# Second attention: rows of queries, keys, sums and low output halves moved by DMA in place of products; out projection in two passes

## Chip, core and metric

The kernel runs on one core of one Trainium2 chip. The metric is the device time of one execution in microseconds; the median of the runs shown counts.

## The reference

The model is a stack of four residual blocks on x of 2 x 1024 tokens x 256 features. The change concerns the third, a causal attention of 16 heads of 16 features:

```python
def _L1_attn_ref(x, w_attn, b_attn, w_proj, b_proj):
    ...
    qkv = x @ w_attn + b_attn
    q, k, v = jnp.split(qkv, 3, axis=-1)
    ...
    q, k, v = (heads(q), heads(k), heads(v))
    scale = 1.0 / np.sqrt(HEAD_DIM).astype(np.float32)
    att = jnp.einsum('bhqd,bhkd->bhqk', q, k) * scale
    causal = jnp.tril(jnp.ones((Tlen, Tlen), dtype=bool))
    att = jnp.where(causal, att, -jnp.inf)
    att = jax.nn.softmax(att, axis=-1)
    y = jnp.einsum('bhqk,bhkd->bhqd', att, v)
    y = y.transpose(0, 2, 1, 3).reshape(Bsz, Tlen, Cdim)
    return y @ w_proj + b_proj
...
x = x + _layernorm(_L1_attn_ref(_layernorm(x, axis=-1), L1_attn_w_attn, L1_attn_b_attn, L1_attn_w_proj, L1_attn_b_proj), axis=-1)
```

The other blocks are an attention of 16 heads of 128 features, a gated feed-forward layer and a mixture of 16 experts. All is in fp32.

## The kernel before

A product with fp32 precision is made of reduced operands: each number is split into a high part (type float32r) and a low part, the rest, and `three_passes` (L78) adds high x high, low x high and high x low. The stages follow each other in blocks, one instruction list per engine, with semaphores between them written by hand. Each engine runs its list in order, so a wait holds all that stands behind it.

The second attention is `attention1_stage` (L1425). Work is cut into 8 **halves**: four heads (`HG`) of one batch. A half has two **chunks** c of 512 queries, and 12 **quads** (c, kt), each the four heads' scores of one chunk against 128 keys. Every engine has a function `step(g)` for the quad g; r = g mod 12 is the step in the half, and `small_work` (L1456) says which small jobs stand at the end of which step, as (kind, half relative to the present one, chunk, part). The steps go from -4 to TOTAL + 10.

What a step does on TensorE (L2002): scores of quad g + 1 for one pair of heads (L1936), the maxima products of unit g + 10 (`maxima`, L1615), weighing v with the exponentials of quad g (`weigh_v`, L1940), then the same for the other pair of heads, then the small jobs (`small`, L1965). Scores and small jobs share a ring of four PSUM banks, maxima use three, o has one. ScalarE takes the exponentials (L2023) and copies o (L2030); GpSimd masks the diagonal quads (`hide_later`, L1870) one step ahead of their weighing; VectorE takes maxima out of PSUM (`take_max`, L1651).

The maxima pass runs one half ahead: unit 0 of the next half stands at r = 2, unit 4 (the first of chunk 1) at r = 6. The small jobs of one half and chunk, in order:

- `project` (L1596): queries and keys of four heads, 128 rows x 512 tokens, six products. ScalarE copies the high part (L1636), VectorE makes the low part (L1648). It stands at r = 11 for chunk 0, two halves ahead, and at r = 3 for chunk 1.
- `stack` (L1602), four per chunk: the scores' operands hold, per head of a pair, high, low and again high (or high, high, low) rows of 16 features above each other, so that one product does all three passes. Two products with a 0/1 matrix `to_stack` place the rows; ScalarE copies them (L1641, L1644). At r = 0, 1 and r = 4, 5.
- `shift` (L1609): the negated maxima are placed in further rows of q and added by VectorE (L1686), at r = 8 and r = 2.
- `sums` (L1985): the sum of exponentials is in o below each head's 16 rows; products with a selector bring it to 128x16, VectorE inverts it (L2094), GpSimd widens it (L1897), `spread` (L1991) transposes it back and ScalarE copies the factor (L2056).
- `make_y` (L1841), GpSimd: multiply o by the factor, high part, low part. Its three instructions stand in three steps (`Y_AFTER`, L1469), with maskings between them.
- `out` (L1994), two per chunk: three passes against the output weights; VectorE adds to the accumulator (L2100).

The first half's projections, stacks and first maxima are made in the block of the first feed-forward layer, at the steps of `early_jobs` (L1476). SP's queue carries only loads here: weights and biases of a half (L1577), constants (L1693).

## Time and profile before

| what | value |
|---|---|
| median of 3 runs | 2309.24 us (2307.34 to 2699.71) |
| profiled execution | 2301.61 us |
| its span | 2299.9 us |
| second attention in the span | 1526 to 1926 us, preparation from 1507 |
| mean granted TensorE clock | 0.962 |
| TensorE, VectorE, ScalarE, GpSimd busy | 2141.7, 1507.0, 1176.5, 541.1 us |

How to read the rows below. A row of a table of stretches has the stretch in us from the span's start, its length, then the busy time (and number of instructions) of TensorE's products, TensorE's weight loads, VectorE, ScalarE and GpSimd, then the granted clock as a share of full speed, the DMA share and GB/s. A timeline row has start, duration, engine (PE TensorE, PEld its weight loads, DVE VectorE, ACT ScalarE, POOL GpSimd, SPq the queue of SP), the line, the operation, what it writes and reads, the shapes, how many are merged in the row, and in brackets the idle time before it and what ended it. Products are pipelined: durations overlap, so what a group costs is read from its start to the start of the next. A row of a group has the count, busy us and mean ns, and the idle time before. In the timeline of TensorE below, steps begin with their first scores (L1936): r = 7 at 1718.49, r = 0 at 1737.42, r = 2 at 1745.54, r = 3 at 1749.20, r = 5 at 1760.12, r = 7 at 1768.07.

### The profile page before, as it was taken

The numbers are of one execution on the slowest core, as the hardware profiler recorded it, in microseconds if no ns is written. First come the engines' busy times: TensorE is split into PE (matmuls) and PEld (weight loads), VectorE is DVE, ScalarE is ACT, GpSimd is POOL, SyncE is SP. The second block draws the span as 40 slices with busy tenths as digits, with TensorE's granted clock in tenths as the row PEclk, the third lists the DMA queues.
The fourth block names the chain that finished last, engine by engine and source line by source line (L and its number), as shares of the span: only waits on it lengthen the run. The fifth ranks groups of instructions, "written<-read, shape, count | busy, mean of one in ns | idle before, by whom it ended". The sixth has DMA issues, their size and how long they took to land. (4 is left out here: it accounts for less than half of the span.)

```text
span 2299.9 us, 36921 instructions
## 1 busy us (share of the span) xinstructions
PE 2141.7 (93%) x12776; PEld 1731.9 (75%) x12776; DVE 1507.0 (66%) x2657; ACT 1176.5 (51%) x2137; POOL 541.1 (24%) x543
## 2 busy tenths in 40 slices
PE   4999999999999999999999979977999987999996
PEld 3888888888888888888888868754555544888885
DVE  4766676676676666767667765456766664566665
ACT  3654565464465555546546555436655664333333
POOL 3012021031031021021020116213434343233332
PEclk8999999999999999999999999988999986899998
DMA  3010010010010010010020010000000000000001
GB/s 79 1 40 2 1 40 2 1 40 2 1 40 2 1 40 2 1 40 2 14 54 1 10 65 10 1 10 3 3 6 3 1 1 21 15 28 21 21 21 37
DMA packets 36811, 39.13 MB, mean 17 GB/s; under 512 B 7712, under 2 KB 33184, under 8 KB 36640
## 3 DMA queue, kind: packets, MB, share of 16 engines
q1 hardware_dynamic: 36640, 36.83, 6.1%
q8 instruction: 110, 1.80, 0.3%
q14 instruction: 61, 0.50, 0.1%
HBM read 34.71 MB, written 2.10 MB: 16 GB/s over the span
## 5 line engine op out<-in xcount | busy, mean ns | idle before, releaser
L735 ACT ACTIVATE attn_probT_hi<-psum 128x512 fp32r<-128x512 f32 x512 | 278.2, 595 | 305.5 <-PE psum L621 305.5
L777 DVE TENSOR_REDUCE attn_neg_max<-psum 128x1 f32<-128x1024 f32 x256 | 313.3, 1224 | 180.1 <-PE psum L81 179.2
L823 DVE TENSOR_TENSOR attn_probT_lo<-psum,attn_probT_hi 128x512 fp32r<-128x512 f32 x512 | 327.6, 682 | 37.7 <-ACT attn_probT_hi L735 37.7
L714 ACT ACTIVATE attn_prob<-psum,attn_neg_max 128x1024 f32<-128x1024 f32 x256 | 286.8, 1120 | 7.2 <-DVE attn_neg_max L777 7.2
L621 PE MATMUL psum<-ident_sb,attn_prob 128*128 128x128 f32 x2048 | 266.7, 273 | 22.0 <-ACT attn_prob L714 12.7
L621 PEld LDWEIGHTS psum<-ident_sb,attn_prob 128*128 128x128 f32 x2048 | 237.1, 140 | 63.2 <-DVE attn_probT_lo L823 13.3
L552 POOL TENSOR_TENSOR attn_v_lo<-x_sb,attn_v_hi 128x512 fp32r<-128x512 f32 x64 | 82.0, 1281 | 766.9 <-ACT attn_v_hi L743 766.9
L2023 ACT ACTIVATE attn_probT<-psum 128x512 f32<-128x512 f32 (+3 forms) x384 | 166.0, 488 | 130.8 <-PE psum L1936 125.9
L81 PE MATMUL psum<-attn_probT_hi,attn_v_hi 128*128 128x512 f32 x512 | 212.2, 414 | 0.6 <-DVE attn_probT_lo L823 0.6
L81 PE MATMUL psum<-attn_key_hi,attn_q_hi 128*128 128x512 f32 x512 | 201.1, 393 | 0.3 <-DVE attn_key_lo L809 0.2
L81 PE MATMUL psum<-attn_probT_lo,attn_v_hi 128*128 128x512 f32 x512 | 201.2, 393 | 0.0
L81 PE MATMUL psum<-attn_key_hi,attn_q_lo 128*128 128x512 f32 x512 | 200.5, 392 | 0.0
L81 PE MATMUL psum<-attn_probT_hi,attn_v_lo 128*128 128x512 f32 x512 | 200.3, 391 | 0.0
L81 PE MATMUL psum<-attn_key_lo,attn_q_hi 128*128 128x512 f32 x512 | 200.2, 391 | 0.0
L1659 DVE TENSOR_REDUCE attn_peaks<-psum 128x1 f32<-128x512 f32 (+1 forms) x256 | 156.2, 652 | 53.1 <-PE psum L1630 30.2
L794 DVE SCALAR_TENSOR_TENSOR acc_sb<-psum,attn_over_total,acc_sb 128x256 f32<-128x256 f32 x256 | 111.7, 478 | 59.2 <-PE psum L81 53.5
L1255 POOL TENSOR_TENSOR moe_hid_lo<-moe_hidden,moe_hid_hi 128x512 fp32r<-128x512 f32 x72 | 93.1, 1293 | 230.1 <-ACT moe_hid_hi L1237 230.1
L81 PE MATMUL psum<-xT_hi,attn_w_hi 128*128 128x512 f32 x288 | 118.4, 411 | 16.8 <-issue 16.8
L1291 DVE TENSOR_TENSOR moe_hidden<-psum,moe_gate_act 128x512 f32<-128x512 f32 x72 | 49.8, 692 | 113.2 <-ACT moe_gate_act L1235 80.8
L81 PE MATMUL psum<-xT_lo,attn_w_hi 128*128 128x512 f32 x288 | 116.7, 405 | 0.0
L81 PE MATMUL psum<-xT_hi,attn_w_lo 128*128 128x512 f32 x288 | 116.5, 405 | 0.0
L81 PE MATMUL psum<-xT_hi,moe_w_hi 128*128 128x512 f32 x288 | 115.5, 401 | 0.5 <-ACT route_score L1374 0.5
(207 smaller groups left out, 4888.5 us busy)
## 6 DMA issues: line engine op xcount, KB each, us to landing
moe_staged<-in_moe_w SPq DMA_DIRECT2D x18, 384.0 KB, 3.0
acc_sb<-in_x SPq DMA_DIRECT2D x4, 512.0 KB, 5.3
x_sb<-in_wq_codes SPq DMA_DIRECT2D x8, 256.0 KB, 2.7
x_sb<-in_wq_scales SPq DMA_DIRECT2D x32, 64.0 KB, 3.0
x_sb<-in_wk_codes SPq DMA_DIRECT2D x8, 256.0 KB, 4.0
x_sb<-in_wk_scales SPq DMA_DIRECT2D x32, 64.0 KB, 4.6
x_sb<-in_wv_codes SPq DMA_DIRECT2D x8, 256.0 KB, 4.9
x_sb<-in_wv_scales SPq DMA_DIRECT2D x32, 64.0 KB, 5.6
```

The lines of the kernel that those rows point to most:

```text
L81: ins = nc.tensor.matmul(out, stationary[s], moving[m], start=start and n == 0, stop=stop and n == len(PASSES) - 1)
L552: nc.gpsimd.tensor_tensor(v[1][:, to, :].rearrange("p t d -> p (t d)"), v_whole[:, n % 2, :], v[0][:, to, :].rearrange("p t d -> p (t d)") ...
L621: mm = nc.tensor.transpose(ring(use)[:, j * P:(j + 1) * P], prob[:, i % 2, kt * P:(kt + 1) * P], k.ident[:])
L714: nc.scalar.activation(prob[:, i % 2, :], scores(i).rearrange("p a b -> p (a b)"), ACT.Exp, bias=neg_max[:, i % 2:i % 2 + 1], accum_out=to ...
L735: nc.scalar.activation(probT[0][:, g % 2, half_tile * GT:(half_tile + 1) * GT, j * P:(j + 1) * P], ring(use).rearrange("p (t n) -> p t n", ...
L777: nc.vector.tensor_reduce(neg_max[:, i % 2:i % 2 + 1], scores(i), AX.XY, ALU.max, negate=True).then_inc(max_ready, 1)
L794: add = nc.vector.scalar_tensor_tensor(out=to, in0=out_bank[:, j * C:(j + 1) * C], scalar=over_total[:, g * GT + t:g * GT + t + 1], in1=to ...
L823: nc.vector.tensor_tensor(to[1], ring(use).rearrange("p (t n) -> p t n", n=P), f32(to[0]), ALU.subtract).then_inc(ring_free, 1)
L1255: nc.gpsimd.tensor_tensor(hid_lo[:, s % 2, :], hidden[:, s % 2, :], hid_hi[:, s % 2, :].bitcast(F32), ALU.subtract).then_inc(lo_done, 1)
L1291: nc.vector.tensor_tensor(h, up_bank(s), g, ALU.mult).then_inc(prod_done, 1)
L1659: nc.vector.tensor_reduce(to[:, h:h + 1], bank[:, 0:width], AX.X, ALU.max, negate=True).then_inc(max_free, 1)
L2023: nc.scalar.activation(probT[:, slot(g, h), q0:], score_bank(g * HG + h)[:, q0:], ACT.Exp, scale=float(D1) ** -0.5).then_inc(exp_done, 1)
```

## The change

Four parts, all in the second attention.

1. `stack` is no longer a job of TensorE. SP issues 24 DMAs per chunk of a half, each of 16 rows x 512 tokens, from the high or low part into q or key. q and key are now one tensor each for both pairs of heads, prepared once with zeros and ones (`set_rows`), by VectorE: for the first buffer in the block before, for the second at the start of this stage. The maxima wait for all 24 moves of their chunk.
2. The sums are moved by four DMAs from below each head's rows of o to the head's rows of `sums`; VectorE inverts 128x512; GpSimd's `make_y` follows in one piece at the same step. `sums`, `spread` and the widening are gone. VectorE's inversion and `make_y` stand at r = 2 (of the half before, chunk 1) and r = 6 (chunk 0).
3. The low part of y is moved by four DMAs below the high part, and the output weights stand in both places: the out projection is two passes.
4. The small jobs are placed anew: `project` of chunk 1 at r = 1 in place of 3, `out` at r = 5, 6 and 9, 10 in place of 6, 7 and 10, 11; the steps end at TOTAL + 7; in the feed-forward block the first maxima stand at steps 15 and 16 where they stood twice at 16. The shift's addition is one instruction of 128x1024, with a factor per row.

SP's order: for half = 0 to 8: stack (half + 1, 0), sums (half - 1, 1), stack (half + 1, 1), low half (half - 1, 1), sums (half, 0), weights (half + 3), low half (half, 0).

```diff
-    LEAD, FIRST, TAIL = 10, 4, 10
+    LEAD, FIRST, TAIL = 10, 4, 7
...
     small_work = {
-        0: [("stack", 1, 0, 0), ("stack", 1, 0, 1)],
-        1: [("stack", 1, 0, 2), ("stack", 1, 0, 3), ("sums", -1, 1, 0)],
+        1: [("project", 1, 1, 0)],
         2: [("shift", 0, 1, 0)],
-        3: [("project", 1, 1, 0), ("spread", -1, 1, 0)],
-        4: [("stack", 1, 1, 0), ("stack", 1, 1, 1)],
-        5: [("stack", 1, 1, 2), ("stack", 1, 1, 3), ("sums", 0, 0, 0)],
-        6: [("out", -1, 1, 0)],
-        7: [("out", -1, 1, 1), ("spread", 0, 0, 0)],
+        5: [("out", -1, 1, 0)],
+        6: [("out", -1, 1, 1)],
         8: [("shift", 1, 0, 0)],
-        10: [("out", 0, 0, 0)],
-        11: [("out", 0, 0, 1), ("project", 2, 0, 0)],
+        9: [("out", 0, 0, 0)],
+        10: [("out", 0, 0, 1)],
+        11: [("project", 2, 0, 0)],
     }
-    Y_AFTER = {(1, 3): 0, (1, 4): 1, (1, 5): 2, (0, 7): 0, (0, 8): 1, (0, 9): 2}
+
+
+    INVERT_AT = {2: (1, 1), 6: (0, 0)}
...
         13: ([], [("project", 0, 0)]),
-        14: ([], [("stack", 0, 0), ("stack", 0, 1)]),
-        15: ([], [("stack", 0, 2), ("stack", 0, 3)]),
-        16: ([("max", 0, 0)], [("max", 1, 0)]),
+        15: ([], [("max", 0, 0)]),
+        16: ([("max", 1, 0)], []),
         17: ([("max", 2, 0)], [("max", 2, 1)]),
         18: ([], [("max", 3, 0)]),
         19: ([("max", 3, 1)], [("project", 1, 0)]),
-        20: ([], [("shift", 0, 0), ("stack", 1, 0)]),
-        21: ([("stack", 1, 1)], [("stack", 1, 2)]),
-        22: ([("stack", 1, 3)], [("max", 4, 0)]),
+        20: ([], [("shift", 0, 0)]),
+        22: ([], [("max", 4, 0)]),
...
+        def stack(sp, of, c):
+
+            sp.wait_ge(qk_lo, of * chunks + c + 1)
+            for which, (to, parts) in enumerate(((q, (0, 1, 0)), (key, (0, 0, 1)))):
+                for h in range(HG):
+                    for n, part in enumerate(parts):
+                        from_row, to_row = (which * HG + h) * D1, h % 2 * ROWS + PARTS_AT[n]
+                        sp.dma_start(f32(to[of % 2][to_row:to_row + D1, h // 2, chunk(c)]),
+                                     f32(qk[part][from_row:from_row + D1, c, :])).then_inc(stacked[c], 16)
+
+        def set_rows(b):
+            nc.vector.memset(f32(q[b][:]), 0.0).then_inc(prepared, 1)
+            nc.vector.tensor_copy(key[b][:], ones_key[:].unsqueeze(2).broadcast_to([P, pairs, SEQ])).then_inc(prepared, 1)
...
+            pe.wait_ge(stacked[c], (half + 1) * STACK)
...
+            to = q[of % 2][:, :, chunk(c)]
+            nc.vector.scalar_tensor_tensor(out=to, in0=f32(to), scalar=keep_rows[:, 0:1],
+                                           in1=misc.unsqueeze(1).broadcast_to([P, pairs, NB]),
+                                           op0=ALU.mult, op1=ALU.add).then_inc(shifted, 1)
...
+            def next_stack(half, c):
+                if half < HALVES:
+                    if half >= 2:
+                        sp.wait_ge(scores_full, (half - 1) * QUADS * HG)
+                    stack(sp, half, c)
+
+            def move_sums(half, c):
+
+                sp.wait_ge(o_done, half * chunks + c + 1)
+                for h in range(HG):
+                    at = h * HEAD_ROWS
+                    sp.dma_start(sums[at:at + D1, c, :], o[at + D1:at + 2 * D1, c, :]).then_inc(sums_ready, 16)
+
+            def move_lo(half, c):
+                sp.wait_ge(y_split, 3 * (half * chunks + c + 1))
+                for h in range(HG):
+                    at = h * HEAD_ROWS
+                    sp.dma_start(f32(y[at + D1:at + 2 * D1, c, :]), f32(y_lo[at:at + D1, :])).then_inc(y_ready, 16)
+
+            for half in range(1, 3):
+                next_weights(half)
+            sp.wait_ge(prepared, 7)
+            for half in range(HALVES + 1):
+                next_stack(half + 1, 0)
+                if half:
+                    move_sums(half - 1, 1)
+                next_stack(half + 1, 1)
+                if half:
+                    move_lo(half - 1, 1)
+                if half < HALVES:
+                    move_sums(half, 0)
+                    next_weights(half + 3)
+                    move_lo(half, 0)
...
+            def make_y(of, c):
+                before_this = of * chunks + c
+                pool.wait_ge(inverted, before_this + 1)
+                nc.gpsimd.tensor_tensor(y_whole[:], o[:, c, :], over_sum[:, c, :], ALU.mult).then_inc(y_split, 1)
+                if of:
+                    pool.wait_ge(misc_full, last_out[before_this - chunks] + 1)
+                pool.wait_ge(y_split, 3 * before_this + 1)
+                nc.gpsimd.tensor_tensor(y[:, c, :], y_whole[:], one[:].broadcast_to([P, NB]), ALU.mult).then_inc(y_split, 1)
+                if before_this:
+                    pool.wait_ge(y_ready, before_this * HG * 16)
+                pool.wait_ge(y_split, 3 * before_this + 2)
+                nc.gpsimd.tensor_tensor(y_lo[:], y_whole[:], f32(y[:, c, :]), ALU.subtract).then_inc(y_split, 1)
...
+                        pe.wait_ge(y_ready, (at + 1) * HG * 16)
                         for j in range(2):
                             t = 2 * part + j
-                            mm = three_passes(nc, misc[:, j * C:(j + 1) * C], [x[:, t * P:(t + 1) * P] for x in y],
-                                              [x[:, of % passes, :] for x in wp])
+                            for half_of in range(2):
+                                mm = nc.tensor.matmul(misc[:, j * C:(j + 1) * C], y[:, c, t * P:(t + 1) * P],
+                                                      wp[half_of][:, of % passes, :], start=half_of == 0, stop=half_of == 1)
...
+            def invert(of, c):
+                dve.wait_ge(sums_ready, (of * chunks + c + 1) * HG * 16)
+                nc.vector.reciprocal(over_sum[:, c, :], sums[:, c, :]).then_inc(inverted, 1)
...
+            nc.vector.memset(sums[:], 1.0).then_inc(prepared, 1)
+            set_rows(1)
...
+    w_proj = np.concatenate([w_proj, w_proj], axis=2)
```

TensorE in a middle half, before, from the end of r = 1 to the first maxima of the next half (`attn_key,attn_q` with 128x128 in L1623) in r = 2; `attn_qk_hi,attn_to_stack` are stacks, L1985 the sums:

```order
L1623 MATMUL psum<-attn_key,attn_q 128x512
L1630 MATMUL psum<-attn_mask,attn_ident_half 128x128 x4
L1605 MATMUL psum<-attn_qk_hi,attn_to_stack 128x512 [waits attn1_qk_lo,attn1_exp_done]
L1605 MATMUL psum<-attn_qk_lo,attn_to_stack 128x512
L1605 MATMUL psum<-attn_qk_hi,attn_to_stack 128x512 [waits attn1_qk_lo,attn1_exp_done]
L1605 MATMUL psum<-attn_qk_lo,attn_to_stack 128x512
L1985 MATMUL psum<-attn_sum_rows,attn_o 128x4 [waits attn1_o_done,attn1_exp_done]
L1985 MATMUL psum<-attn_sum_rows,attn_o 128x4 x3
L1936 MATMUL psum<-attn_q,attn_key 128x128 [waits attn1_exp_done]
L1936 MATMUL psum<-attn_q,attn_key 128x128 [waits attn1_misc_free3]
L1623 MATMUL psum<-attn_key,attn_q 128x128 [waits attn1_stacked,attn1_max_free]
L1623 MATMUL psum<-attn_key,attn_q 128x128
```

The same place after; L81 with `attn_w` is the projection of chunk 1, L1628 the maxima:

```order
L81 MATMUL psum<-xT_hi,attn_w_hi 128x512 [waits norm2_lo_done,attn1_w_ready,attn1_exp_done]
L81 MATMUL psum<-xT_lo,attn_w_hi 128x512
L81 MATMUL psum<-xT_hi,attn_w_lo 128x512
L81 MATMUL psum<-xT_hi,attn_w_hi 128x512
L81 MATMUL psum<-xT_lo,attn_w_hi 128x512
L81 MATMUL psum<-xT_hi,attn_w_lo 128x512
L1950 MATMUL psum<-attn_q,attn_key 128x128 [waits attn1_exp_done] x2
L1628 MATMUL psum<-attn_key,attn_q 128x128 [waits attn1_stacked0,attn1_max_free]
L1628 MATMUL psum<-attn_key,attn_q 128x128
L1635 MATMUL psum<-attn_mask,attn_ident_half 128x128 x4
L1628 MATMUL psum<-attn_key,attn_q 128x128 x2
L1635 MATMUL psum<-attn_mask,attn_ident_half 128x128 x4
```

The stacks and sums are gone from r = 1, the projection has come there, and the first maxima now wait for `stacked0`, the moves of SP.

GpSimd in a middle half, before, from the end of r = 6 (the weights' split, L1583, L1585) on; L1879 is the masking of a diagonal quad, L1846, L1851 and L1854 make y:

```order
L1879 AFFINE_SELECT attn_probT<-attn_probT 128x2x128 [waits attn1_w_ready,attn1_exp_done]
L1879 AFFINE_SELECT attn_probT<-attn_probT 128x2x128 [waits attn1_exp_done]
L1846 TENSOR_TENSOR attn_wide<-attn_o,attn_wide 128x512 [waits attn1_spread_done]
L1879 AFFINE_SELECT attn_probT<-attn_probT 128x2x128 [waits attn1_exp_done] x2
L1851 TENSOR_TENSOR attn_y_hi<-attn_wide,attn_one 128x512 [waits attn1_y_split,attn1_misc_full]
L1879 AFFINE_SELECT attn_probT<-attn_probT 128x2x128 [waits attn1_exp_done] x2
L1865 TENSOR_TENSOR attn_v<-attn_v_all,attn_one 128x32x16 [waits attn1_weighed]
L1854 TENSOR_TENSOR attn_y_lo<-attn_wide,attn_y_hi 128x512 [waits attn1_y_split]
L1879 AFFINE_SELECT attn_probT<-attn_probT 128x2x128 [waits attn1_y_split,attn1_exp_done]
```

The same place after; L1869, L1873 and L1877 make y, L1900 is the masking:

```order
L1589 TENSOR_TENSOR attn_bias<-attn_bias_in,attn_one 128x1 [waits attn1_qk_lo,attn1_landed]
L1581 TENSOR_TENSOR attn_w_hi<-attn_w_in,attn_one 128x256
L1583 TENSOR_TENSOR attn_w_lo<-attn_w_in,attn_w_hi 128x256 [waits attn1_split]
L1869 TENSOR_TENSOR attn_y_whole<-attn_o,attn_over_sum 128x512 [waits attn1_w_ready,attn1_inverted]
L1873 TENSOR_TENSOR attn_y<-attn_y_whole,attn_one 128x512 [waits attn1_y_split,attn1_misc_full]
L1877 TENSOR_TENSOR attn_y_lo<-attn_y_whole,attn_y 128x512 [waits attn1_y_split,attn1_y_ready]
L1900 AFFINE_SELECT attn_probT<-attn_probT 128x2x128 [waits attn1_exp_done] x6
```

The three instructions that make y stood between the maskings of quads 8 to 11, the first behind that of quad 8; now all three stand ahead of the masking of quad 8, and the first of them waits for VectorE's inversion of the same step.

## Rows read from the trace of the kernel before

**Rows 1.** Table of stretches: the first, one middle and the last half.

```profile
1526.00:1577.00 51.00, 41.25 (x284) 20.96 (x282) 36.31 (x83) 31.18 (x66) 13.83 (x24) 0.87 0.01 3
...
1723.00:1770.00 47.00, 43.00 (x338) 24.88 (x330) 31.35 (x57) 27.59 (x59) 17.24 (x27) 0.93 0.01 4
1870.00:1926.00 56.00, 44.76 (x285) 22.49 (x285) 30.59 (x76) 33.11 (x78) 26.19 (x40) 0.76 0.01 1
```

**Rows 2.** Waits from 1526 to 1926 us: total, times, longest.

```profile
ACT attn_probT L2023 <- PE psum L1936: 125.9, 116, 16.9
```

**Rows 3.** Timeline of TensorE from r = 7 (1718.49) to r = 7.

```profile
1718.49 0.50 PE L1936 MATMUL psum<-attn_q,attn_key 64*128 64x512 f32 x2
...
1720.78 0.38 PE L81 MATMUL psum<-attn_wp_hi,attn_y_hi 128*128 128x256 f32 x1
...
1721.59 0.60 PE L1991 MATMUL psum<-ident_sb,attn_wide 128*128 128x128 f32 x4
...
1737.42 0.45 PE L1936 MATMUL psum<-attn_q,attn_key 64*128 64x384 f32 x2
...
1745.54 0.33 PE L1936 MATMUL psum<-attn_q,attn_key 64*128 64x128 f32 x2
1746.31 0.33 PE L1623 MATMUL psum<-attn_key,attn_q 64*128 64x128 f32 x2 [0.44 <-ACT attn_key L1641]
...
1749.20 0.80 PE L1936 MATMUL psum<-attn_q,attn_key 64*128 64x512 f32 x2 [0.78 <-DVE attn_q L1686]
...
1758.99 0.50 PE L1605 MATMUL psum<-attn_qk_hi,attn_to_stack 128*128 128x512 f32 x1
...
1760.12 0.50 PE L1936 MATMUL psum<-attn_q,attn_key 64*128 64x512 f32 x2
...
1763.72 0.95 PE L1985 MATMUL psum<-attn_sum_rows,attn_o 128*128 128x4 f32 x8
...
1768.07 0.50 PE L1936 MATMUL psum<-attn_q,attn_key 64*128 64x512 f32 x2
```

**Rows 4.** Timeline of SP's queue.

```profile
9.83 3.89 SPq L479 DMA_DIRECT2D x_sb<-in_wv_scales  x4
...
1375.15 0.43 SPq L1696 DMA_DIRECT2D attn_in_ident_half<-in_ident_half  x1
1375.62 0.43 SPq L1696 DMA_DIRECT2D attn_ones_key<-in_ones_key  x1
...
1507.85 0.33 SPq L1832 DMA_DIRECT2D attn_sum_rows<-in_sum_rows  x1
```

**Rows 5.** DMA issues: size, median us from issue to landing.

```profile
attn_sum_rows<-in_sum_rows SPq DMA_DIRECT2D x1, 2.0 KB, 1.6
```

**Rows 6.** Timeline of VectorE: low part after the projection.

```profile
1738.24 0.75 DVE L1648 SCALAR_TENSOR_TENSOR attn_qk_lo<-psum,attn_bias,attn_qk_hi 128x512 fp32r<-128x512 f32 x1 [1.40 <-ACT attn_qk_hi L1636]
```

**Rows 7.** Groups of VectorE: reciprocals from SBUF, and a cast.

```profile
L788 DVE RECIPROCAL attn_over_total<-attn_total 128x4 f32<-128x4 f32 x64 | 10.8, 169 | 0.0
...
L1763 DVE CAST attn_to_stack<-attn_in_to_stack 128x1024 fp32r<-128x1024 f32 x1 | 0.9, 862 | 0.0
...
L1400 DVE RECIPROCAL route_factor<-route_total 128x16 f32<-128x16 f32 x1 | 0.3, 253 | 0.0
```

**Rows 8.** Timeline of the last output of the stage.

```profile
1925.02 0.60 ACT L2030 ACTIVATE attn_o<-psum 128x512 f32<-128x512 f32 x1 [1.81 <-PE psum L1953]
...
1930.05 1.26 POOL L1846 TENSOR_TENSOR attn_wide<-attn_o,attn_wide 128x512 f32<-128x512 f32 x1 [1.48 <-ACT attn_wide L2056]
...
1934.03 0.55 PE L81 MATMUL psum<-attn_wp_hi,attn_y_hi 128*128 128x256 f32 x1 [4.69 <-POOLq L1856]
...
1936.97 0.69 DVE L2100 TENSOR_TENSOR acc_sb<-acc_sb,psum 128x512 f32<-128x512 f32 x1 [0.59 <-PE psum L81]
```

**Rows 9.** Timeline of TensorE in the feed-forward block.

```profile
1446.52 0.39 PE L81 MATMUL psum<-xT_hi,attn_w_hi 128*128 128x512 f32 x1
...
1457.34 0.40 PE L1605 MATMUL psum<-attn_qk_hi,attn_to_stack 128*128 128x512 f32 x1
```

158 lines of the change are left out of this document (41 added, 117 removed).

## Prediction

> **What bounds the kernel now.** I read the table of stretches first, then the waits inside the second attention, then its timeline, engine by engine. The stage runs from 1526 to 1926 us. Seven of its eight halves ("half": four heads of one batch) take 344 us together, 49.1 us each, at a granted clock of 0.87 in the first and 0.93 in one of the middle; the eighth, with no maxima to prepare, takes 56 us at 0.76 [rows 1]. No engine is full: TensorE is busy 81 to 91% of a half by durations that overlap, VectorE 31 to 36 us of it, ScalarE 28 to 31. The waits of the stage show who waits for whom: first stands ScalarE's exponential, 125.9 us behind TensorE's scores [rows 2]. So work taken off TensorE shortens a half nearly by its length, as long as nothing new is waited for: TensorE's queue is in order, and a wait on it holds scores, exponentials and weighing together. I number steps in a half r = 0 to 11.
>
> **What goes from TensorE.** A step with two stack pieces spends 1.13 us on them (1758.99 to 1760.12), and there are four such steps: 4.5 us. Sums take 0.95 us (their row at 1763.72), 0.9 up to the next product, twice; spreading 0.60, 0.5 up to the next, twice; six products of an out piece take 0.81 us (1720.78 to 1721.59), so the third pass is 0.27 in each of four pieces, 1.0 [rows 3]. Together 8.3 us a half. ScalarE's copies of stacks and factors and GpSimd's widening go too; ScalarE has 17 us or more idle in a half [rows 1] and hides them, so I count them at nothing.
>
> **What a move costs.** In its place SP issues 24 moves for one chunk of one half, 48 a half, with 8 moves of sums, 8 of low halves and 2 loads: 66. On SP's queue small DMAs start 0.475 us apart (1375.15, 1375.62) and four large ones in a row took 3.89 us, 0.97 each [rows 4]. A 2 KB by 16 move inside SBUF is not in the trace; its price is bounded by 0.33, the shortest issue of a load (of the sums' selector, after a pause), and 0.97, and I take 0.475: the two rows are of 128 KB and 1 KB and cost the same. That selector, 2 KB, landed 1.6 us after its issue [rows 5]; for 32 KB I take 2.0. A chunk is then 24 x 0.475 = 11.4 us of issuing.
>
> The Trainium skill, page "DMA: Bandwidth & Descriptors", section "Issuing engines are not separate DMA queues", says that the time a sequencer needs to initiate a DMA is usually small beside the DMA. By that the moves would run as one burst of some 2 us, which is the second rival below. Here the issue row (0.43 us) is a fifth of the landing, and 24 in a row outweigh it fivefold. By its rule table the other way ("Many small transfers": coalesce, under 64 KB one pays mostly overhead) a move of 32 KB is overhead, which agrees with these rows.
>
> **The wait at the head of maxima.** Time 0 is the end of the projection for the next half's chunk 0, at the end of r = 11. The copy and the low half end 1.6 us later (1737.42 to 1738.99) [rows 6]. Issuing ends at 13.0, the last move, issued at 12.5, has landed at 14.5. TensorE needs these rows for the first maxima, which stand at r = 2, unchanged: there are only r = 0 and r = 1 (8.1 us before, 1737.42 to 1745.54, less two stack steps and the sums, plus 1.5 for the projection that moved there: 6.4) and 0.3 of scores [rows 3]. It arrives at 6.7 and waits 7.8 us. Before, these rows came from TensorE and ScalarE, with a wait of 0.44 us [rows 3]. Queued behind are weighing, scores and the shift.
>
> **The reciprocal.** It was 128x16 (0.257 us) and is 128x512. Two rows from SBUF give the slope: 4 elements 0.169, 16 elements 0.253, so 7.0 ns each and 3.7 us for 512 [rows 7]; with the semaphore 3.8. Its bounds are the cast of 1024 elements at its rate, 0.43 us for 512, and 512/16 of the 16-element row, 8.1; I stay with the slope, which the same operation gives. The Trainium skill, "VectorE: DVE Perf Modes", section "First, the fixed hardware budget", says that the reciprocal is an iterative divide with a repeat count of 8; as an estimate by the page's 0.96 GHz that is 8.3 ns an element, 4.3 us, and the sum would grow by about 1 us a half.
>
> **The half, step by step.** After 14.5: the rest of r = 2, 1.9 us (3.7, less 0.8 before its first maxima and a wait of 0.8 at its end, less the scores), and 1.0 more because TensorE has stood idle for 7.8 us: after the pause at 1749.20 the same pair of scores takes 0.80 us that takes 0.50 elsewhere [rows 3]. That is 17.4. The shift's addition (1.3) ends at 18.7, then VectorE's reciprocal, whose sums landed at 16.3, to 22.5. TensorE does r = 3 (1.8: r = 3 and 4 took 10.9 before, 1749.20 to 1760.12, less 2.7 projection, 0.8 spreading and 1.1 stack, 6.3, with r = 3 at the low pace; at the full one I take 1.8 and 3.2) and comes to the maxima of r = 4 at 20.8; with three banks it needs a maximum that VectorE takes after the reciprocal, at 23.2: 2.4 us lost. r = 4 ends at 26.4. GpSimd's three steps (the first begins at 1930.05, TensorE goes on at 1934.03; 3.8 without the signal) [rows 8] end at 26.3; SP has issued chunk 1 by 26.2 and then moves the low halves, landed at 29.7; TensorE's out projection at r = 5 has come at 28.9 and waits 0.8. r = 5 ends at 30.3, r = 6 at 33.6 (the two were 7.95 long before, 1760.12 to 1768.07, and become 6.3). Now the second reciprocal (34.3 to 38.1), then GpSimd's three to 41.9. They stand in one block ahead of the masking of quad 8, which before stood in front of the first and between the others; two maskings (0.9) end at 42.8. The steps r = 7 to 11 took 18.9 us (1718.49 to 1737.42), of it 1.6 projecting v, which only two halves do, 1.4 waits, 0.5 spreading and 0.7 third pass: 14.7 remain. Of these TensorE has done 3.3 at 36.9, where it wants to weigh quad 8: 5.9 us lost. The other 11.4 end at **54.2 us**, against 49.1. Waits of 7.8 + 1.0 + 2.4 + 0.8 + 5.9 = 17.9 us have eaten the 8.3 and the small waits of before that fall into them.
>
> **The sum**, against the profiled execution (2301.6 us, span 2299.9, 1.7 around it):
> - seven halves x 5.1: +35.7.
> - last half: no stack; sums, spreading and third pass go (3.8, colder: 5), the r = 6 wait comes (5.9): +1.
> - its end: from the copy of o (1925.62) to the last addition (1937.66) it was 12.0 us [rows 8]; it becomes 3.5 (move and landing) + 3.8 + 3.8 + 3.5 + 2.7: +5.
> - start: VectorE fills sums, q and key for the second buffer ahead of its first maximum: 1024 + 2048 + 2048 elements at the rate of the cast of 1024 (0.862 us) [rows 7] are 4.3 us, little of it hidden: +4.
> - the first feed-forward stage: the projection begins at 1446.5 and takes 1.6, its rows would be there 14.5 later, at 1462.6; the first maxima now stand where the second stacks stood, 1457.3, or 1456.2 without the first, and wait some 6.4 us; 16 stack products go (3.7, at 0.23 each where they stand among others of their kind) [rows 3, 9]: +2.7.
> Together +48.4: 2350.0 for the profiled execution. The median of the runs shown (2309.2) lies 7.6 above that execution, and I add it: **2358**, 2.1% slower. About 2% is what a measurement of this kernel can tell from no change.
>
> **Rivals.**
> First: not slower. Issue at 0.37, between the two lowest rows, landing at 1.6 and a reciprocal of 0.7 us, the rate of plain operations. The maxima then wait 5.3, r = 4 nothing, r = 8 about 2.7; the half is 46 us. 7 x -3.1 = -22, last half and early stage -1, end +2, start +4: -17, **2292**. For it speaks the issue of 0.33 us after a pause; against it the two reciprocal rows. It decides below some 7.5 us for 24 moves together with under 1.5 us for a reciprocal.
> Second: faster. If moves inside SBUF issue at 0.13 us or less, the rows land before r = 2 and the reciprocals hide: 7 x -8.3 and -5 elsewhere, **2246**. No issue of SP's in these rows is below 0.33.
> Third: SP's queue is the bound. At 0.97 a move, 66 issues are 64 us a half: 7 x 14.9, and 14 + 8 + 4 + 1 more for early stage, end, start and last half: +131, **2441**. The rows at 0.97 stand behind megabytes of loads; a move here is 32 KB, so against it.
> Fourth: the clock. The stack pieces were dense full-array products; the half with the fewest, the last, was granted 0.76 [rows 1]. If the others go from 0.93 to 0.75, some 31 us of products a half grow by 8, half of it inside waits: +28, **2386**. The Trainium skill, "TensorE: Matmul & The Clock Gate", section "HAM oscillation — how this bites in real kernels", describes waits for DMA that bring back the low clock with every round; the rows at half pace above agree that pauses do so here.
>
> **Chances.** Forecast 0.50, its own range 2330 to 2395; first rival 0.20, second 0.08, third 0.12, fourth 0.10. Of the forecast, somewhat more than half lies beyond 2355. Slower by over 2%: 0.28 + 0.12 + 0.10 = 0.50; faster 0.08; within 2% 0.42. The range leaves out the second rival and the far end of the third: 2285 to 2430.
>
> **What would show it.** In the profile after: TensorE idle some 8 us before the 128-wide maxima, seven times, released by a DMA into q or key; SP's moves 0.475 us apart; reciprocals near 3.7 us; TensorE idle before weighing quad 8, released by the masking, with GpSimd behind the reciprocal; halves of 54 us. The forecast is wrong if moves start under 0.3 us apart, if the reciprocal takes under 1.5 us, or if halves come below 49 us; if SP never rests, the third rival holds.

## The result, and the profile after

The changed kernel takes 2491.1 us (median; 2488.3 to 2496.2), against 2308.3 for the one before: ratio 1.080, 95% interval 1.077 to 1.083. One of the four runs of the kernel before (2699.7) was in a slower state and is left out of the ratio. Forecast were 2358 us and a range of 2285 to 2430. Slower was right; the loss is 183 us, not 49. The profiled execution has a span of 2486.6 us, 186.7 more than before.

First where the time went. VectorE's low parts of the projections mark the same place in both kernels; this is its timeline after, for the first half's two chunks and the second half's first:

```profile
1453.28 0.75 DVE L1647 SCALAR_TENSOR_TENSOR attn_qk_lo<-psum,attn_bias,attn_qk_hi 128x512 fp32r<-128x512 f32 x1 [1.27 <-ACT attn_qk_hi L1643]
...
1502.74 0.75 DVE L1647 SCALAR_TENSOR_TENSOR attn_qk_lo<-psum,attn_bias,attn_qk_hi 128x512 fp32r<-128x512 f32 x1 [1.37 <-ACT attn_qk_hi L1643]
...
1554.27 0.75 DVE L1647 SCALAR_TENSOR_TENSOR attn_qk_lo<-psum,attn_bias,attn_qk_hi 128x512 fp32r<-128x512 f32 x1 [1.30 <-ACT attn_qk_hi L1643]
```

Before, the three stood at 1448.85, 1487.59 and 1532.62. Further on ScalarE's copies of o mark the ends of halves six, seven and eight (counted from one), at 1980.68 (before 1833.92), 2050.03 (1879.37) and 2105.91 (1925.02), and the stage's last addition ends at 2124.29 (1937.66).

| stretch | before | after | more | forecast |
|---|---|---|---|---|
| up to the first projection | 1448.85 | 1453.28 | 4.4 | 0 |
| to chunk 1's projection (feed-forward block) | 38.7 | 49.5 | 10.7 | 2.7 |
| to the second half's first projection | 45.0 | 51.5 | 6.5 | 4 |
| six halves | 301.3 | 426.4 | 125.1 | 30.6 |
| seventh half | 45.5 | 69.4 | 23.9 | 5.1 |
| last half | 45.7 | 55.9 | 10.2 | 1 |
| end | 12.6 | 18.4 | 5.7 | 5 |

So 80% of the loss is that a half takes 71 us where it took 50 and was forecast at 54. Stretches of the changed kernel (columns as in [rows 1]: length, busy time of PE, PEld, DVE, ACT and POOL, granted clock, DMA share, GB/s): one half with v's projection, then one without, then the last.

```profile
1767.00:1838.00 71.00, 48.02 (x316) 24.37 (x308) 38.33 (x57) 22.08 (x51) 15.89 (x26) 0.74 0.14 32
1838.00:1909.00 71.00, 48.22 (x292) 23.09 (x292) 37.12 (x55) 22.17 (x52) 15.93 (x26) 0.66 0.14 32
...
2050.00:2105.90 55.90, 34.89 (x176) 13.28 (x174) 27.98 (x62) 26.90 (x63) 18.59 (x29) 0.59 0.04 10
```

TensorE has fewer products than before and is busy for longer; the granted clock is 0.66 to 0.74 where [rows 1] had 0.93. The same over halves two to seven, from one of ScalarE's copies of o to another, before and after:

```profile
1590.95:1879.37 288.42, 266.63 (x2093) 154.42 (x2094) 193.03 (x348) 178.54 (x380) 105.91 (x164) 0.95 0.01 3
```
```profile
1626.03:2050.03 424.00, 285.94 (x1808) 140.37 (x1808) 228.77 (x336) 139.61 (x320) 94.59 (x152) 0.70 0.14 32
```

What TensorE waits for, in the timeline of TensorE from r = 2 of one half to its r = 8:

```profile
1772.67 0.33 PE L1950 MATMUL psum<-attn_q,attn_key 64*128 64x128 f32 x2
1783.84 0.47 PE L1628 MATMUL psum<-attn_key,attn_q 64*128 64x128 f32 x2 [10.84 <-DMA attn_key<-attn_qk_lo]
...
1788.84 0.80 PE L1950 MATMUL psum<-attn_q,attn_key 64*128 64x512 f32 x2 [1.38 <-DVE attn_q L1684]
...
1792.88 0.69 PE L1628 MATMUL psum<-attn_key,attn_q 64*128 64x384 f32 x2 [0.50 <-DVE attn_peaks L1655]
...
1804.51 0.36 PE L2000 MATMUL psum<-attn_wp_hi,attn_y 128*128 128x256 f32 x1 [2.80 <-DMA attn_y<-attn_y_lo]
...
1815.74 0.49 PE L1628 MATMUL psum<-attn_key,attn_q 64*128 64x512 f32 x2 [2.10 <-DVE attn_peaks L1655]
1820.12 1.93 PE L1967 MATMUL psum<-attn_probT,attn_v 128*32 128x512 f32 x8 [3.88 <-POOL attn_probT L1900]
```

All four waits of the forecast are there, at their places: 10.84 for the rows (forecast 7.8), 0.50 at r = 4 for a maximum behind the reciprocal (2.4), 2.80 for the low halves (0.8), and 2.10 + 3.88 at r = 8 (5.9). The timeline of SP's queue in the same half:

```profile
1766.93 0.51 SPq L1607 DMA_DIRECT2D attn_q<-attn_qk_hi  x1
1767.48 0.59 SPq L1607 DMA_DIRECT2D attn_q<-attn_qk_lo  x1
...
1782.37 2.48 SPq L1841 DMA_DIRECT2D attn_sums<-attn_o  x4
1784.95 0.53 SPq L1607 DMA_DIRECT2D attn_q<-attn_qk_hi  x1
...
1800.06 2.48 SPq L1847 DMA_DIRECT2D attn_y<-attn_y_lo  x4
1802.59 2.49 SPq L1841 DMA_DIRECT2D attn_sums<-attn_o  x4
1805.12 0.58 SPq L1577 DMA_DIRECT2D attn_w_in<-in_w_attn  x1
...
1819.37 2.41 SPq L1847 DMA_DIRECT2D attn_y<-attn_y_lo  x4
...
1838.53 0.51 SPq L1607 DMA_DIRECT2D attn_q<-attn_qk_hi  x1
```

24 moves of rows, 4 of sums, 24 of rows and 4 of low halves stand without a gap from 1766.93 to 1802.54: 35.6 us for 56, that is 0.636 each from start to start, where 0.475 was assumed. The low halves land 2 us later, and the out projection at r = 5 starts at 1804.51: **37.6 us after the first move, all of it SP's queue**. A whole half is 71.6; over its last 34 us SP issues for 4.0.

The third thing is the clock. In stretches of 4 us of the table of stretches (granted clock 1.00 is the upper of the two levels, 2.4 GHz, and 0.50 the lower, 1.2), the half of before that [rows 3] show is at the lower level for 6.8 us (around 1747 to 1755), this half for some 37 us, most of it from the wait at r = 2 to r = 5 and again behind the wait for the masking. On average over halves two to seven it is 5.1 us of a half before and 43 us after, added up from the granted clock of stretches of 1 us. Three rows of this half (stretches of 4 us) show the fall, with TensorE idle in the last two:

```profile
1770.00:1774.00 4.00, 3.00 (x24) 1.65 (x16) 3.34 (x8) 1.68 (x5) 0.54 (x2) 1.00 0.22 49
1774.00:1778.00 4.00, 0.00 (x0) 0.00 (x0) 0.25 (x1) 0.00 (x0) 0.28 (x1) 0.93 0.24 52
1778.00:1782.00 4.00, 0.00 (x0) 0.00 (x0) 0.00 (x0) 0.00 (x0) 0.00 (x0) 0.50 0.24 53
```

The products say the same: weighing v by eight products takes 1.06 us at 1766.61 and 1.93 at 1820.12.

### The profile page after: what moved, and what is told of

Its sections match the earlier page's. It is cut to its first block and busy times, and to the rows that moved or that the text cites. A ratio compares the mean times of both kernels' runs of the same rounds, so it can differ in the third digit from the quotient of the medians.

```text
span 2486.6 us, 36396 instructions
## 1 busy us (share of the span) xinstructions
PE 2162.3 (87%) x12392; PEld 1714.9 (69%) x12392; DVE 1560.8 (63%) x2645; ACT 1125.7 (45%) x2057; POOL 528.6 (21%) x527
## 5 line engine op out<-in xcount | busy, mean ns | idle before, releaser
L823 DVE TENSOR_TENSOR attn_probT_lo<-psum,attn_probT_hi 128x512 fp32r<-128x512 f32 x512 | 327.6, 682 | 37.9 <-ACT attn_probT_hi L735 37.8
L1628 PE MATMUL psum<-attn_key,attn_q 64*128 64x512 f32 (+3 forms) x384 | 96.1, 500 | 135.6 <-DMA attn_key<-attn_qk_lo 86.3
L81 PE MATMUL psum<-attn_probT_hi,attn_v_hi 128*128 128x512 f32 x512 | 212.6, 415 | 0.6 <-DVE attn_probT_lo L823 0.6
L81 PE MATMUL psum<-attn_probT_lo,attn_v_hi 128*128 128x512 f32 x512 | 201.5, 394 | 0.0
L81 PE MATMUL psum<-attn_key_hi,attn_q_hi 128*128 128x512 f32 x512 | 200.9, 392 | 0.2 <-DVE attn_key_lo L809 0.2
L81 PE MATMUL psum<-attn_probT_hi,attn_v_lo 128*128 128x512 f32 x512 | 200.7, 392 | 0.0
L81 PE MATMUL psum<-attn_key_hi,attn_q_lo 128*128 128x512 f32 x512 | 200.5, 392 | 0.0
L81 PE MATMUL psum<-attn_key_lo,attn_q_hi 128*128 128x512 f32 x512 | 200.2, 391 | 0.0
L1967 PE MATMUL psum<-attn_probT,attn_v 128*32 128x512 f32 (+3 forms) x768 | 121.7, 720 | 52.6 <-POOL attn_probT L1900 36.8
L1628 PEld LDWEIGHTS psum<-attn_key,attn_q 64*128 64x128 f32 x384 | 51.1, 260 | 158.4 <-issue 89.0
L81 PE MATMUL psum<-xT_hi,attn_w_hi 128*128 128x512 f32 x288 | 117.8, 409 | 15.2 <-issue 15.2
L1950 PEld LDWEIGHTS psum<-attn_q,attn_key 64*128 64x128 f32 x384 | 47.3, 247 | 120.9 <-issue 81.1
```

Of the source, the lines that this page charges most:

```text
L81: ins = nc.tensor.matmul(out, stationary[s], moving[m], start=start and n == 0, stop=stop and n == len(PASSES) - 1)
L823: nc.vector.tensor_tensor(to[1], ring(use).rearrange("p (t n) -> p t n", n=P), f32(to[0]), ALU.subtract).then_inc(ring_free, 1)
L1628: mm = nc.tensor.matmul(to[h], q[half % 2][rows(h), pair, t * P:(t + 1) * P], key[half % 2][rows(h), pair, keys], start=True, stop=not uni ...
L1967: mm = nc.tensor.matmul(o_bank[h * HEAD_ROWS:(h + 1) * HEAD_ROWS, q0:], v[half % 2][:, kt, h, :], probT[:, slot(g, h), q0:], start=kt == 0 ...
```

## The experiments

The theory after the first reading: the moves' wait at r = 2 and the clock that falls in it. Rivals: the clock falls because the stack products are gone; the loss is in the sums and low halves. Where no ratio is given, a time below is that of a single run; before's own runs beside them lie between 2302 and 2312 us.

**Projection earlier.**

```
-        8: [("shift", 1, 0, 0)],
+        8: [("shift", 1, 0, 0), ("project", 2, 0, 0)],
...
-        11: [("project", 2, 0, 0)],
```

> One edit on the changed kernel: the projection of the next-but-one half's first chunk stands at r = 8 (behind the shift) instead of r = 11, so its 24 moves may start some 12 us earlier and their 17 us (24 x 0.632 + 2.0) end before TensorE wants them at r = 2. Theory (the wait for the moves, and the slow clock that the idle TensorE brings back, make the half 71 us instead of 54): the wait of 10.8 us goes, and about half of the 12 us by which products got slower: 6 or 7 halves x 17 us, 2385 us against 2491. Rival A (the clock is low because the dense stack products are gone, whatever is waited for): only the wait goes, 70 us, 2420, and the granted clock of a middle half stays near 0.7. Rival B (SP's queue or the low-half moves are the bound): the moves start no earlier than now, under 20 us gained, 2470 or more.

2431.3 us: a miss by 46, and 11 from rival A's 2420. The projection did come early (low part at 1798.52), but the first move stands at 1803.30: q and key have two buffers, so the moves must wait for this half's last scores. They start 5 us earlier, the wait is 5.35 in the half shown, and the halves take 60 to 66 us. Their granted clock is 0.71 to 0.78, about what rival A asked for; but the wait is only halved, so the run doesn't decide between that rival and the theory. From the first move to the out projection of r = 5 it is again 37.8 us:

```profile
1803.30 0.51 SPq L1606 DMA_DIRECT2D attn_q<-attn_qk_hi  x1
```
```profile
1819.83 0.47 PE L1627 MATMUL psum<-attn_key,attn_q 64*128 64x128 f32 x2 [5.35 <-DMA attn_key<-attn_qk_lo]
...
1841.12 0.36 PE L1999 MATMUL psum<-attn_wp_hi,attn_y 128*128 128x256 f32 x1 [3.25 <-DMA attn_y<-attn_y_lo]
```

**Filler in the wait.**

```
+                if half and n == 0 and pair_of_fills == 0:
+                    for i in range(40):
+                        nc.tensor.matmul(max_bank(fill), wp[0][:, 0, 0:P], flat(wp[0][:])[:, 0:NB], start=True, stop=True)
                 maxima(pe, half, n, pair_of_fills, [max_bank(fill + h) for h in range(2)])
```

> One edit on the changed kernel: ahead of the first maxima of each half (not of the first half) TensorE does 40 additional dense full-array products of 512 columns (0.235 us apart, 9.4 us) into the bank that the maxima are about to fill; their results are not used. They lie in the wait of 10.8 us for the moves. Theory (the products behind the wait are slow because TensorE stood idle and its granted clock fell): the rest of the half runs at the full level, busy time of a half without the filler falls from 48 to about 40 us, seven halves x 8 us: 2435 us. Rival C (they are slow because DMA traffic or another engine disturbs them): nothing is gained, 2490 to 2495.

2491.1 us, nothing gained. That is rival C's number, but not its mechanism. Timeline of TensorE behind the filler:

```profile
1704.98 9.36 PE L1940 MATMUL psum<-attn_wp_hi 128*128 128x512 f32 x40
1715.95 0.33 PE L1628 MATMUL psum<-attn_key,attn_q 64*128 64x128 f32 x2 [1.60 <-DMA attn_key<-attn_qk_lo]
...
1737.19 0.55 PE L2003 MATMUL psum<-attn_wp_hi,attn_y 128*128 128x256 f32 x1 [5.32 <-DMA attn_y<-attn_y_lo]
```

The maxima behind it take 0.33 us instead of 0.47 with the same moves in flight, so the idle time is what slowed them. The fast pace lasts only until 1719, where the clock falls behind the wait for the shift. TensorE comes to the out projection some 2 us sooner after the maxima than without the filler. But the time gained went into the next wait, 5.32 us for the low halves instead of 2.80: the first move stood at 1698.96, and 38.2 us later comes the out projection. So the slow products of r = 2 to 5, as far as this run made them faster, cost nothing by themselves; SP's 56 moves cover them. What the slow products behind r = 5 cost it doesn't show: they stay slow in it. That run turned the theory: not the wait at r = 2 but the whole order of moves up to r = 5 is the bound there.

**One part at a time.** The first kernel places rows by products again, at the steps of before; in the second only the rows are moved, with `sums`, `spread`, `make_y` and the three passes of before:

```
+        0: [("stack", 1, 0, 0), ("stack", 1, 0, 1)],
+        1: [("stack", 1, 0, 2), ("stack", 1, 0, 3)],
...
+        3: [("project", 1, 1, 0)],
+        4: [("stack", 1, 1, 0), ("stack", 1, 1, 1)],
```

> Undoes one part of the change: the rows of queries and keys are placed by TensorE's products and ScalarE's copies again, where they stood before; the sums, the low output halves and the two passes stay as changed. Theory: the wait for moves at r = 2 is gone and the clock comes back to about 0.9; what is left of the change is the reciprocal of 512 elements and GpSimd's block ahead of the masking of quad 8 (6 us a half) and a wait of 1 to 3 us for the low halves, less 3.8 us of products: the half 52 to 55 us, 2335 to 2360. Rival D (the sums and low halves cost nothing, all the loss is in the stack): the half 46 us, 2285. Rival E (these cost most of the loss): over 2430.

> The other part alone: rows of queries and keys go by 24 moves a chunk, with the changed layout of q and key; sums, reciprocal of 16 elements, spreading, widening and the out projection in three passes are as before. Theory: a wait of 10 us at r = 2 in each half and products at half pace behind it, less 4.5 us of stack products: half about 62 us, and the whole loss of 17 us in the feed-forward block: 2410. Rival D (all the loss is in the stack): 2490. Rival E: under 2350.

2377.4 and 2389.5 us, 69 and 81 more than before (2308.1): the first 17 above the range given, the second 20 below its number, and neither near rival D or E. Both parts cost, and together (183) 32 more than their sum. That fits with one queue that carries 56 moves in a row only when both are there; it was not tested by itself. In the first TensorE still loses 2.4 us a half at a maximum behind the reciprocal and 3.9 at the masking of quad 8:

```profile
1808.98 0.50 PE L1625 MATMUL psum<-attn_key,attn_q 64*128 64x512 f32 x2 [2.38 <-DVE attn_peaks L1658]
1813.35 1.94 PE L1969 MATMUL psum<-attn_probT,attn_v 128*32 128x512 f32 x8 [3.87 <-POOL attn_probT L1902]
```

**Fewer moves, the same bytes.**

```
-                    for n, part in enumerate(parts):
-                        from_row, to_row = (which * HG + h) * D1, h % 2 * ROWS + PARTS_AT[n]
+                    for n, part in ((0, 0), (2, parts[2])):
+                        count = 2 * D1 if n == 0 else D1
```

> On the changed kernel: the two pieces of a head that lie next to each other (rows 0 to 31 of its block) are moved by one DMA of 32 rows in place of two of 16, so a chunk has 16 moves in place of 24 with the same bytes. The second piece is then not the right one: the rows that carry low halves of queries hold a neighbour's high rows, and the scores are computed from them. Theory, as the first runs leave it (in three kernels the time from the first move of a chunk to the out projection at r = 5 is 37.6 us, which is 56 issues on SP's queue x 0.632 + 2.1 landing, so SP's order of moves sets the first half of a half): a chunk is 10.1 us of issuing, the wait at r = 2 falls from 10.8 to 5.7, that at r = 5 goes, the half is 62 to 64 us and the kernel 2410 to 2435. Rival F (the bytes or the landing set the pace): 2480 or more, with moves of 64 KB landing twice as late.

2408.9 us, 1 us below the theory's range, with halves of 56 to 64 us; far from rival F. The rows are there 12.5 us after the first move (1731.52 to 1744.05) instead of 16.9, and a move of 64 KB lands as soon as one of 32 (DMA issues: size, median us to landing):

```profile
attn_key<-attn_qk_hi SPq DMA_DIRECT2D x64, 64.0 KB, 2.0
...
attn_key<-attn_qk_lo SPq DMA_DIRECT2D x64, 32.0 KB, 2.0
```

A move of 64 KB is also issued in the same 0.63 us. Bytes don't matter here, the number of issues does: 16 fewer of them a half gave 82 us in all, and the lower level of the clock lasts 31 us of a half instead of 43.

**Another queue for 8 of the 56, and y behind the masking.** In the first kernel `move_sums` and `move_lo` are issued in GpSimd's program; in the second:

```
-    INVERT_AT = {2: (1, 1), 6: (0, 0)}
+    INVERT_AT, Y_AT = {2: (1, 1), 6: (0, 0)}, {2: (1, 1), 7: (0, 0)}
```

> On the changed kernel: the 4 moves of sums and the 4 of low halves are issued by GpSimd instead of SP (sums at r = 4 and r = 0, low halves right behind the three steps that make them). SP then issues only the 48 moves of rows and the loads. Theory (SP's queue of 56 moves): the low halves no longer stand behind chunk 1, the wait of 2.8 us at r = 5 goes, the one of 10.8 at r = 2 stays: half 68 us, 2470. Rival G (GpSimd pays more for each move than SP and has the maskings behind it): the low-half moves stand ahead of the masking of quad 8, which wait grows from 3.9 us by four issues: 2490 to 2540.

> On the changed kernel: GpSimd makes y of chunk 0 at r = 7, behind the masking of quad 8, instead of r = 6 ahead of it; VectorE's reciprocal stays. Theory (GpSimd's block ahead of the masking holds the weighing of quad 8): the wait of 3.9 us before it goes in all eight halves, the low halves land some 2 us before the out projection at r = 9 wants them: 2491 - 31 = 2460. Rival H (the wait moves to the out projection at r = 9, or the clock is what holds this stretch): 2480 or more.

2479.6 us, between its two numbers, and 2452.2, 8 below the theory's and further from rival H. In the first the wait for low halves is all but gone from the list of TensorE's waits (3.0 us in the seven halves), and that for the masking grew from 36.8 us in all to 57.9, since four issues stand ahead of it; so rival G holds for that part, while its price does not: four issues take GpSimd 1.98 us, SP 2.48. In the second the masking wait is down to 2.7 us outside the last half (9.7 there), and the out projections wait for low halves more often (25.2 us in eleven waits, before 18.2 in six), which is what rival H had.

**Reciprocal earlier, without the rows' moves.** On the kernel with stack products:

```
-    INVERT_AT = {2: (1, 1), 6: (0, 0)}
+    INVERT_AT = {2: (1, 1), 5: (0, 0)}
```

> On the kernel whose rows are placed by products again (2377 us): the reciprocal of chunk 0 and GpSimd's three steps stand at r = 5 instead of r = 6, since with an almost empty SP queue the sums land by then. Theory: the reciprocal (3.35 us) and the three steps (3.8) end before quad 8 is to be masked, its wait of 6.3 us (2.4 + 3.9) goes, and with it the slow products behind it (1 to 3 us a half): 8 x 7 to 9 us, 2305 to 2320. Rival I (VectorE waits for the sums at r = 5 and TensorE for its maxima): 2350 or more. Rival J (the two remaining parts gain what TensorE gave up, 3.8 us a half): 2285.

2343.1 us, ratio 1.016 (1.012 to 1.019): half of what was hoped. The wait for the masking shrank to 1.2 us where the trace was read, but the maxima still wait 2.0 to 2.6 for the reciprocal, and halves two to seven take 48 to 55 us.

**Three buffers.** They need 16 KB more a partition, which is there. The first kernel has nothing else, the second moves only the rows, the third is the changed kernel with all repairs:

```
-                        sp.wait_ge(scores_full, (half - 1) * QUADS * HG)
+                        sp.wait_ge(scores_full, (half - 2) * QUADS * HG)
...
-        1: [("project", 1, 1, 0)],
+        0: [("project", 1, 1, 0)],
...
+        8: [("shift", 1, 0, 0), ("project", 2, 0, 0)],
```

> On the changed kernel: q and key have three buffers in place of two, so the moves of the next-but-one half's first chunk need not wait for the last scores of this half; its projection stands at r = 8, chunk 1's at r = 0 in place of 1. Nothing else. Theory (in the run with the projection alone at r = 8 the first move stood behind the last scores, 5 us ahead of where it was instead of 12; SP's queue of 56 to 66 issues at 0.632 is then the next bound, 41.7 us of it a half): the wait of 10.8 at r = 2 goes wholly, the masking wait of 6 and the low-half wait at r = 5 stay: half 54 to 58 us, 2370 to 2400. Rival K (something other than the order of moves holds r = 2, such as the DMA traffic beside the products): 2430 or more, as with the projection alone.

> The kernel in which only rows of queries and keys are moved (2390 us; sums, spreading and three passes as before), with the three buffers, chunk 0 projected at r = 8 and chunk 1 at r = 0. Theory: 48 issues of 30.3 us a half have room beside a half of 45 us, no wait for moves is left in the attention stage, and the half is what it was before less the 4.5 us of stack products, 45 to 46 us; the loss of some 15 us in the feed-forward block (the first chunk's 24 moves have no lead there) and 4 us of fills stay: 2309 - 7 x 4 + 19 = 2300, range 2285 to 2320. Rival L (without stack products the granted clock falls and the half stays near 49): 2325 or more.

> The changed kernel with all that the runs so far pointed to: three buffers with the projections at r = 8 and r = 0, sums and low halves issued by GpSimd, y of chunk 0 made behind the masking of quad 8, its out projection at r = 10 and 11. The reciprocals of 512 elements stay. Theory: no wait above 3 us is left in a half; TensorE's 8.3 us come through less about 3 us for VectorE's reciprocal ahead of maxima: half 44 to 46 us, minus 28 against before, plus 22 for the feed-forward block, fills and the end: 2300, range 2285 to 2325. Rival M (VectorE, with 6.7 us more of reciprocals, or GpSimd, with 8 us of issues, is the next bound): half 50 us or more, 2340.

2422.4, 2319.8 (ratio 1.0055, 1.0039 to 1.0071) and 2367.9 us (1.027, 1.025 to 1.030): all later than the theory's number, the second at its range's upper end. In the first the wait at r = 2 fell to 1.72 us and that for low halves rose to 5.02, with the 56 moves still ahead of them; the queue is the bound again. In the second the queue is not: halves two to seven take 47.2 us each, of before 48.1, though 4.5 us of products are gone from each. It is the nearest of the kernels run; none beats the kernel before. In the third no single wait rules: over its stage the masking, the moves (of rows and low halves) and the maxima behind a reciprocal take 19 to 23 us each, a half is 52 us, and rival M is the nearer, though 28 us off. Table of stretches, halves two to seven of the second kernel (those of before are shown above):

```profile
1611.63:1895.05 283.42, 258.79 (x2002) 143.43 (x2002) 193.32 (x338) 147.74 (x333) 105.88 (x164) 0.87 0.15 34
```

In these six halves 27 us of products are gone (6 x 4.5), but TensorE's busy time fell by 7.8 us only (266.63 to 258.79): the other products take 19 us more. The granted clock says why, 0.87 where before had 0.95: the lower level lasts 12.7 us of a half instead of 5.1. That is the fourth rival's sign, so:

**Idle products put back.**

```
+        0: [("fill", 1, 0, 0), ("fill", 1, 0, 1), ("project", 1, 1, 0)],
...
+                    elif kind == "fill":
+                        for _ in range(2):
+                            mm = nc.tensor.matmul(misc, wp[0][:, 0, 0:P], flat(wp[0][:])[:, 0:NB], start=True, stop=True)
...
+                    if kind == "fill":
+                        pe.wait_ge(misc_full, use + 1)
+                        pe.nop().then_inc(small_free(use), 1)
```

> The kernel with only the rows moved and three buffers (1.0055 of before), in which the 16 dense full-array products a half that placed the rows before (two a piece, two pieces each at r = 0, 1, 4 and 5) are put back as work whose results nobody uses, each pair into a bank of the ring. It asks what taking 4.5 us of products from TensorE is worth when no move is waited for. Theory N (a product off TensorE shortens the half by its length, as the prediction had it): they cost 16 x 0.235 = 3.8 us a half and 28 us in all, 2347 us, ratio 1.017 to 1.018. Rival P (they were paid back by the clock: with them the pauses are shorter, the granted clock of a middle half goes from 0.80 to 0.87 back to about 0.93 and the other products run faster): at most a third of that, ratio 1.005 to 1.009.

2366.7 us, ratio 1.027 (1.025 to 1.028): above both. Halves two to seven grew from 47.2 to 53.8 us. A pair of fillers holds TensorE for 0.9 us (1731.22 to 1732.11 below), and the eight of a half for 7.4; the stack's pieces held it for 0.56 each [rows 3]. The difference is in the edit's last three lines: behind each pair TensorE waits for the end of its own products, which it did not behind a piece of the stack. Two such products 0.235 us apart are 0.47 us; the rest of the 0.9 is this wait.

```profile
1731.22 0.73 PE L1987 MATMUL psum<-attn_wp_hi 128*128 128x512 f32 x2
1732.11 0.70 PE L1987 MATMUL psum<-attn_wp_hi 128*128 128x512 f32 x2
1733.10 0.48 PE L81 MATMUL psum<-xT_hi,attn_w_hi 128*128 128x512 f32 x1 [0.30 <-PE psum L1987]
```
```profile
1620.73:1943.62 322.89, 293.98 (x2099) 158.33 (x2098) 194.19 (x338) 148.35 (x333) 106.08 (x164) 0.87 0.13 30
```

And the fillers did not bring the clock back: over the six halves it is 0.87 with them and 0.87 without. So 6.6 of the 7.4 us that they hold are lost, but half of that is the wait that only this edit has, and what rival P is about, a clock that returns, did not come. The run decides neither for theory N nor against rival P; what the stack's own products are worth stays open.

## Why the prediction was wrong, step by step

Two steps failed: the price of issuing a move, and the term for the clock. The waits themselves were the right ones, but larger; what follows goes through the terms of the sum in order.

- **What goes from TensorE, 8.3 us a half.** The count was right: over halves two to seven the records have 285 products fewer (2093 to 1808), 47.5 a half. That it shortens a half "nearly by its length, as long as nothing new is waited for" was not: with the rows' wait gone and 4.5 us of products off, a half gained 0.8. By the rows, 3.2 of the missing 3.7 us are in slower products, at a clock that is low for 7.6 us longer. Why it is low longer was not settled.
- **What a move costs, 0.475 us: this step failed.** It took 0.636. The bounds (0.33 and 0.97) held it, but the value was taken from loads [rows 4], and it enters the half 56 times ahead of the out projection of r = 5: 56 x 0.16 = 9.0 us of the 17.4 by which the half is longer than forecast (71.6 against 54.2). The landing, 2.0, was exact. The Trainium skill says on page "DMA: Bandwidth & Descriptors", section "Issuing engines are not separate DMA queues", that the time to initiate is usually small beside the DMA. The runs disagree for small moves in a row: one issue, 0.63 us, is already a third of its landing, and 56 of them are 35.6 us of issuing with 2.0 of landing; the run with fewer, larger moves shows that the number of issues and not the bytes sets it.
- **The wait at the head of maxima, 7.8 us.** It was 10.8. The rows came 3.9 us later by that same term (24 x 0.16); TensorE came 1.0 later than the forecast's 6.7 us behind the projection (1765.27 to 1773.00).
- **The low halves at r = 5.** Forecast were 28.1 us from first move to out projection (1.6 to 29.7), and there were 37.6. The working had the right chain, that chunk 1 and the low halves stand in SP's queue, and took TensorE to be nearly as late by itself. The third rival (SP's queue is the bound) was given 0.12 at 0.97 a move. Its mechanism holds from r = 0 to 5 already at 0.636, where SP is busy for only 41.5 of the 71.6 us of a half: a queue needn't be full to be the bound, it need only be full ahead of a dated wait.
- **Reciprocal, 3.7 us.** It took 3.35, 6.5 ns an element; the slope of the same operation was a good measure, and GpSimd's block, 5.9 us lost at the masking, came as 2.1 + 3.9. The 2.4 us at r = 4 were 0.5. Moving y behind the masking gave 39 us back.
- **The half behind r = 5** was to be 26.1 us (29.7 to 54.2, and 1.6 to the next move) and took 34.0. The wait was right. In this half 3.1 of the 7.9 us are the projection of v, which two halves have and the forecast's half has not; in the next half, without it, the stretch takes 33.7 us all the same (1876.45 to 1910.11). There TensorE is busy for 20 us at the lower level, which at half pace is 10 us lost, and here for 12. So **the second step that failed is the term for the clock**: 1.0 us was put down for it in a half. Over halves two to seven TensorE's busy time is 285.9 us where before's 266.6 less the forecast's 8.3 a half would be 216.8: slower products, 11.5 us a half. Up to r = 5 they lie beside SP's queue, behind it they lengthen the half. No run has the changed kernel with a fast clock behind r = 5, so this share is read from the rows and not shown by an edit. The fourth rival named the mechanism at 0.10 and 4 us a half; it came on top of the forecast, not in its place. The Trainium skill, "TensorE: Matmul & The Clock Gate", section "HAM oscillation — how this bites in real kernels", describes DMA waits that bring the low clock back in each round. The rows agree for the wait at r = 2 (0.93 in its second stretch of 4 us, 0.50 in its third), and so does the run with filler, in which the first products behind the same wait were fast.
- **Feed-forward block, 2.7 us.** There were 4.4 + 10.7. Of the 10.7, the wait for the moves is 9.8 instead of 6.4, again the issue; the products behind it (1470.73 to 1477.21, some at half pace) take 2.8 us more than the same ones before, for which the sum had no term; the eight stack products of this stretch give 1.9 back. The fills of q and key (1.76 and 1.16 us on VectorE) stand here for the first buffer too; the sum had them for the second only. If all of that is in the 4.4, some 1.5 us of it are not accounted for. The start, 4 us, was 6.5 and was not taken apart.
- **Last half, 1 us.** It lost 10.2. GpSimd's statistics for the next stage stand behind its three steps; ScalarE waits for them ahead of the copy of o, and TensorE for that copy, 8.45 us:

```profile
2069.58 2.07 ACT L252 ACTIVATE acc_sb<-acc_sb,room_sb 128x256 f32<-128x256 f32 x4 [5.44 <-POOL room_sb L213]
2071.56 0.57 ACT L2032 ACTIVATE attn_o<-psum 128x512 f32<-128x512 f32 x1
```
```profile
2072.19 1.93 PE L1967 MATMUL psum<-attn_probT,attn_v 128*32 128x512 f32 x8 [8.45 <-ACT attn_o L2032]
```

- **End of the stage, 5 us**: 5.7.

Most of the errors have one sign. A reading that fits is that the terms were chained: a longer issue makes a longer wait, which lowers the clock, which lengthens what stands behind the next wait. The run with fewer moves agrees as far as it goes: with 10 us less of issuing a half, the lower level is 12 us shorter. That the time lay beyond the upper bound, and not only beyond the forecast, took both failed steps: the issue's 9.0 us alone, in seven halves, would give 2358 + 63 = 2421.

## What to carry to other kernels

When many small DMAs take over work of an engine, count the issues on one queue between two points that are waited for, at the price of a run of such moves (here 0.63 us each, for 32 KB as for 64), and ask from when the target buffer is free: two buffers, not the projection, set the start here. A wait put into TensorE's queue costs its length and, where nothing else is the bound, the half pace behind it. Products removed from TensorE can be worth less than their length: here 4.5 us of them gave 0.8, since the others became slower. Order the slow helpers (a wide reciprocal, y on GpSimd) behind the maskings that the next product waits for.
